# A fused retention and feed-forward block: small matmul tiles of two batches in one stretch, outputs in banks of their own, another order behind it

## The reference

```python
xn = layernorm(x)                                   # no weights
q, k, v = xn @ Wq, xn @ Wk, xn @ Wv                 # 8 heads of 16 features
# retention, in chunks of 64 tokens, gamma differs by head:
attn = einsum('bhid,bhjd->bhij', qc, kc) * D        # D[i,j] = gamma**(i-j) for i >= j, else 0
o_intra = einsum('bhij,bhje->bhie', attn, vc)
o_inter = einsum('bhid,bhde->bhie', qc * decay_q, S)
S = decay_s * S + einsum('bhjd,bhje->bhde', kc * decay_k, vc)
o = (o_intra + o_inter) @ Wo
h = ternary(w_fc) * scale applied to xn + gate * (xn @ v.T @ fast_b.T @ u.T)
y = ternary(w_proj) * scale applied to relu(h) ** 2
out = x + o + y
```

## Time and profile before

| what | value |
|---|---|
| median of 3 runs | 129.23 us (128.18 to 129.38) |
| the profiled execution's own time | 129.01 us |
| its span, first to last instruction | 127.0 us |
| granted TensorE clock, mean | 0.997 |
| PE busy | 117.0 us (92%) |
| DVE busy | 99.2 us (78%) |
| ACT busy | 78.7 us (62%) |
| POOL busy | 64.0 us (50%) |
| the chain that ended last | PE 80%, DVE 10%, issue 4%, ACT 2%, POOL 1% |

### The profile page before, as it was taken

How to read it: one execution, slowest core, us unless ns; L and a number is a source line. 1 busy time by engine, 2 the same in 40 slices (tenths; PEclk the granted TensorE clock), 3 DMA queues, 4 the chain that set the end, 5 groups by cost and what they waited for, 6 DMA issues and landing times.

```text
span 127.0 us, 6564 instructions
## 1 busy us (share of the span) xinstructions
PE 117.0 (92%) x2860; PEld 92.8 (73%) x2860; DVE 99.2 (78%) x261; ACT 78.7 (62%) x158; POOL 64.0 (50%) x60
## 2 busy tenths in 40 slices
PE   4979999988999999499999999999999999499991
PEld 4425869856688778377788778878897889377890
DVE  0788795489799969858699979896999799729832
ACT  3265669967871897227972897188738774382910
POOL 7099803984439161923439252916193529544400
PEclk9999999999999999999999999999999999999998
DMA  3849920000023000400023001300020002000202
GB/s 105 296 149 320 389 92 34 0 3 5 8 90 81 5 0 23 145 7 0 0 92 74 0 0 53 112 0 0 0 83 0 0 0 83 0 5 0 88 5 83
DMA packets 3357, 7.71 MB, mean 61 GB/s; under 512 B 384, under 2 KB 896, under 8 KB 3216
## 3 DMA queue, kind: packets, MB, share of 16 engines
q1 hardware_dynamic: 2880, 7.01, 16.3%
q10 hardware_dynamic: 464, 0.50, 1.2%
HBM read 5.42 MB, written 2.10 MB: 59 GB/s over the span
## 4 chain that ended last, share of the span: by engine, by line
PE 80%; DVE 10%; issue 4%; ACT 2%; POOL 1%; DVEq 0%; POOLq 0%
PE ps_work L659 10%; PE ps_score L735 8%; PE ps_work L663 7%; PE ps_work L660 7%; PE ps_score L705 6%; PE ps_score L747 5%; PE ps_score L781 5%; PE ps_y L761 4%; PE ps_y L762 4%; PE ps_score L720 3%; DVE sums_of L532 3%; PE ps_turn L668 3%; PE ps_y L765 2%; DVE xn L491 2%; PE ps_turn L692 1%
## 5 line engine op out<-in xcount | busy, mean ns | idle before, releaser
L300 POOL TENSOR_TENSOR sq_lo<-square,sq_hi 128x512 fp32r<-128x512 f32 x31 | 39.8, 1295 | 36.2 <-ACT sq_hi L356 36.2
L347 ACT ACTIVATE square<-ps_work 128x512 f32<-128x512 f32 x32 | 19.1, 596 | 23.1 <-PE ps_work L663 22.6
L516 DVE TENSOR_TENSOR scores<-ps_score,cst 128x512 f32<-128x512 f32 x32 | 20.3, 682 | 1.6 <-PE ps_score L705 1.6
L305 POOL TENSOR_TENSOR q_pair<-q_dec,cst 128x1024 f32<-128x1024 f32 x7 | 13.3, 1894 | 15.9 <-DVE q_dec L501 15.9
L356 ACT ACTIVATE sq_hi<-square 128x512 fp32r<-128x512 f32 x32 | 20.1, 627 | 0.1
L352 ACT ACTIVATE square<-square 128x512 f32<-128x512 f32 x32 | 18.9, 630 | 0.1
L491 DVE TENSOR_SCALAR xn<-x_in,mean_var,rstd 128x128 f32<-128x128 f32 x32 | 14.9, 528 | 0.3
L659 PE MATMUL ps_work<-xn_hi,w_hi 128*128 128x512 f32 x32 | 14.3, 447 | 0.4 <-issue 0.4
L735 PE MATMUL ps_score<-scores,v_pad 64*32 64x64 f32 x1024 | 12.5, 225 | 1.6 <-issue 1.6
L663 PE MATMUL ps_work<-xn_lo,w_hi 128*128 128x512 f32 x32 | 12.6, 394 | 0.0
L660 PE MATMUL ps_work<-xn_hi,w_lo 128*128 128x512 f32 x32 | 12.6, 393 | 0.0
(11 more groups left out here) (123 smaller groups left out, 238.6 us busy)
## 6 DMA issues: line engine op xcount, KB each, us to landing
x_in<-x_tok SPq DMA_DIRECT2D x8, 256.0 KB, 3.4
resid<-x_feat SPq DMA_DIRECT2D x1, 2048.0 KB, 7.7
out_feat<-resid SPq DMA_DIRECT2D x7, 256.0 KB
po_in<-ffn_weights SPq DMA_DIRECT2D x1, 320.0 KB, 3.2
fc_in<-ffn_weights SPq DMA_DIRECT2D x1, 256.0 KB, 3.7
q_table<-q_decay SPq DMA_DIRECT2D x1, 256.0 KB, 3.5
wqvk<-qvk_weights ACTq DMA_DIRECT2D x1, 192.0 KB, 3.9
cst<-const ACTq DMA_DIRECT2D x1, 129.0 KB, 3.9
```

Of the source, the lines that this page charges most:

```text
L300: nc.gpsimd.tensor_tensor(sq_lo[p][:, f, :], square[p][:, f, :], sq_hi[p][:, f, :].bitcast(F32), ALU.subtract).then_inc(lo_ready, 1)
L347: nc.scalar.activation(square[b.parity][:, f, :], ps_work[f % 2][:], ACT.Relu).then_inc(relu_ready, 1)
L516: nc.vector.tensor_tensor(scores[:, g].rearrange("p t s i -> p (t s) i"), ps_score[:, g].rearrange("p (a i) -> p a i", i=BLK), causal.unsq ...
```

## The change

The small tiles of two batches are put into one stretch: score(b), gather_states(b), own_values(b-1), carry(b-1). own_values moves a batch later, so there are two score tiles in SBUF (`scores` by parity). Outputs and states get two PSUM banks of their own (`ps_out`: the output in the first 256 columns of each, the states behind it); `ps_turn` and `ps_y` become banks 2 and 3 of `ps_score`, and keys and values of the tokens go to banks 0 and 1. All four hidden tiles stand ahead of the stretch. Behind it come the second product of b-1, the turned xn of b+1, the output product of b-1, and queries, keys and values of b+1. The queues of ScalarE and VectorE follow; GpSimd's and SyncE's stay. The waits change with the banks.

```diff
-        scores = sb("scores", [P, NG, NT, PAIR, BLK])
+        scores = [sb(f"scores{p}", [P, NG, NT, PAIR, BLK]) for p in range(2)]
...
         ps_score = pb("ps_score", [P, NG, SEQ])
+        ps_out = pb("ps_out", [P, ROWS, SEQ])
         ps_work = [pb(f"ps_work{p}", [P, SEQ]) for p in range(2)]
-        ps_turn = pb("ps_turn", [P, SEQ])
-        ps_y = pb("ps_y", [P, SEQ])
+        ps_turn, ps_y = ps_score[:, 2], ps_score[:, 3]
+        first_turn, ps_w1 = ps_out[:, 0], ps_out[:, 1]
...
             def body(b):          # ScalarE
                 take_relu(b, 0)
                 take_relu(b, 1)
                 root(b.step(1))
-                take_square(b, 0)
-                take_square(b, 1)
-                high_square(b, 0)
+                take_relu(b, 2)
+                take_relu(b, 3)
+                for f in range(3):
+                    take_square(b, f)
+                    high_square(b, f)
                 high_o(b.step(-1))
-                take_relu(b, 2)
-                high_square(b, 1)
                 round_xn(b.step(1))
-                take_relu(b, 3)
-                take_square(b, 2)
                 take_square(b, 3)
-                high_square(b, 2)
+                high_square(b, 3)
                 copy_k(b.step(1))
                 copy_k_tok(b.step(1), 0)
-                high_square(b, 3)
                 copy_k_tok(b.step(1), 1)
...
             def body(b):          # VectorE
                 before, after = b.step(-1), b.step(1)
                 statistics(after)
                 statistics_done(after)
-                take_states(before)
+                take_v(b, 1)
                 variance(after)
-                for k in range(3):
-                    add_states(before, k)
                 for step in range(4):
                     inverse_root(after, step)
                 normalise(after)
+                for g in MASK_ORDER:
+                    mask_scores(b, g)
                 low_o(before)
                 low_xn(after)
-                for g in MASK_ORDER[:2]:
-                    mask_scores(b, g)
+                take_states(b)
+                for k in range(3):
+                    add_states(b, k)
+                decay_q(after)
                 finish(before, ps_y)
-                decay_q(after)
-                for g in MASK_ORDER[2:]:
-                    mask_scores(b, g)
-                for side in range(2):
-                    take_v(after, side)
+                take_v(after, 0)
...
             def turn_xn(b):       # TensorE
                 pe.wait_ge(xn_ready, b.count(1, 1))
+                if b is not first:
+                    pe.wait_ge(scores_ready, b.count(NG, 1 - NG))
...
             def project_vk(b, side):
-                if side == 1 and b is first:
+                if b is not first:
+                    pe.wait_ge(scores_ready, b.count(NG, 0))
+                elif side == 1:
                     pe.wait_ge(q_ready, b.count(1, 1))
-                elif side == 1:
-                    pe.wait_ge(y_free, b.count(1, 0))
...
             def score(b):
                 pe.wait_ge(k_ready, b.count(1, 1))
                 pe.wait_ge(q_spread, b.count(PAIR, PAIR))
+                if b is not first:
+                    pe.wait_ge(v_ready, b.count(2, 2))
+                    pe.wait_ge(y_free, b.count(1, 0))
...
-            def body(b):
-                before, after = b.step(-1), b.step(1)
+            def all_hidden(b):
                 pe.wait_ge(q_ready, b.count(1, 1))
                 hidden(b, 0)
                 pe.wait_ge(k_ready, b.count(1, 1))
-                hidden(b, 1)
-                pe.wait_ge(v_ready, b.count(2, 2))
+                for f in range(1, NF):
+                    hidden(b, f)
+
+            def small_tiles(b):
+                before = b.step(-1)
+                pe.wait_ge(scores_ready, before.count(NG, NG))
+                pe.wait_ge(state_ready, before.count(1, 1))
+                score(b)
+                gather_states(b)
+                own_values(before)
+                carry(before)
+
+            def body(b):
+                before, after = b.step(-1), b.step(1)
+                all_hidden(b)
+                small_tiles(b)
+                pe.wait_ge(scores_ready, b.count(NG, 2))
                 second_product(before, ps_y, range(NF))
-                carry(before)
-                hidden(b, 2)
-                hidden(b, 3)
                 turn_xn(after)
                 pe.wait_ge(o_lo_ready, before.count(1, 1))
-                score(b)
                 output_product(before, ps_y)
                 project_q(after, b)
                 project_k(after, b)
                 project_vk(after, 0)
                 project_vk(after, 1)
-                gather_states(b)
-                own_values(b)
...
             before = last.step(-1)
-            pe.wait_ge(q_ready, last.count(1, 1))
-            hidden(last, 0)
-            carry(before)
-            pe.wait_ge(k_ready, last.count(1, 1))
-            hidden(last, 1)
-            pe.wait_ge(v_ready, last.count(2, 2))
-            second_product(before, ps_y, range(0, 2))
+            all_hidden(last)
+            small_tiles(last)
+            pe.wait_ge(scores_ready, last.count(NG, 2))
+            second_product(before, ps_y, range(NF))
             pe.wait_ge(o_lo_ready, before.count(1, 1))
-            score(last)
-            second_product(before, ps_y, range(2, NF))
+            own_values(last)
             output_product(before, ps_y)
-            hidden(last, 2)
-            for _ in range(6):
-                mm(ps_turn[0:GW, 0:1], ident[0:GW, 0:GW], ident[0:GW, 0:1], start=True, stop=True)
-            gather_states(last)
-            hidden(last, 3)
-            pe.wait_ge(relu_ready, last.count(NF, 3))
             last_second(0)
             last_second(1)
-            own_values(last)
             carry(last)
             last_second(2)
             last_second(3)
```

More of the change, by code:

```diff
@@ L204, in v_slots, with turn_bank @@
             return v.rearrange("p t g (s e) -> p (t g) s e", e=DK)[:, :, 0:4:3, :]
+        def turn_bank(b):
+            return first_turn if b is first else ps_turn
         def vk_bank(b, side):
-            other = ps_work[0] if b is first else ps_y
-            return (ps_turn if side == 0 else other)[:].rearrange("p (w t d) -> p w t d", w=2, t=2)
+            if b is first:
+                bank = first_turn if side == 0 else ps_work[0][:]
+            else:
+                bank = ps_score[:, side]
+            return bank.rearrange("p (w t d) -> p w t d", w=2, t=2)
         def by_block(o):
             return o[:].rearrange("p (t r i) -> p t r i", r=ROWS, i=BLK)
-        o_bank = ps_score[:, 0:ROWS, 0:NT * BLK].rearrange("p r (t i) -> p t r i", i=BLK)
+        o_bank = ps_out[:, :, 0:NT * BLK].rearrange("p r (t i) -> p t r i", i=BLK)
+        state_bank = ps_out[:, :, NT * BLK:NT * (BLK + GW)]
         first, last = Batch(0, 0), Batch(NB // 2 - 1, 1)
         HALF = SEQ // 2
-        last_banks = [ps_turn, ps_work[0]]
+        last_banks = [ps_score[:, 0], ps_score[:, 1]]
         last_cols = [slice(last.index * SEQ + h * HALF, last.index * SEQ + (h + 1) * HALF) for h in range(2)]
@@ L496, in low_xn @@
                 dve.wait_ge(xn_hi_ready, b.count(1, 1))
-                nc.vector.tensor_tensor(xn_lo[:], ps_turn[:], xn_hi[:].bitcast(F32), ALU.subtract).then_inc(xn_lo_ready, 1)
+                nc.vector.tensor_tensor(xn_lo[:], turn_bank(b), xn_hi[:].bitcast(F32), ALU.subtract).then_inc(xn_lo_ready, 1)
             def decay_q(b):
@@ L543, in finish @@
                 cols = bass.ds(b.index * SEQ, SEQ)
-                nc.vector.scalar_tensor_tensor(out=resid[:, cols], in0=bank[:], scalar=scale[:, NF:NF + 1],
+                nc.vector.scalar_tensor_tensor(out=resid[:, cols], in0=bank, scalar=scale[:, NF:NF + 1],
                                                in1=resid[:, cols], op0=ALU.mult, op1=ALU.add).then_inc(y_free, 1)
@@ L598, in _ @@
             nc.vector.tensor_tensor(wo_lo[:], ps_y[:, 0:D], wo_hi[:].bitcast(F32), ALU.subtract).then_inc(y_free, 1)
+            take_states(first)
+            for k in range(3):
+                add_states(first, k)
             take_v(after, 0)
-            take_v(after, 1)
             dve.wait_ge(resid_loaded, 16)
@@ L632, in _ @@
             before = last.step(-1)
-            take_states(before)
-            for k in range(3):
-                add_states(before, k)
-            low_o(before)
+            take_v(last, 1)
             for g in MASK_ORDER:
                 mask_scores(last, g)
-            finish(before, ps_y)
+            low_o(before)
             take_states(last)
@@ L647, in _ @@
                                     ALU.subtract).then_inc(last_low_ready, 1)
+            finish(before, ps_y)
             dve.wait_ge(o_done, last.count(1, 1))
@@ L734, in own_values @@
                                 rows = slice(r * BLK, (r + 1) * BLK)
```

(17 more changed lines are left out.)

63 lines of the change are left out of this document (33 added, 30 removed).

## The result

The kernel after takes 140.43 us, the median of four runs (139.83 to 144.58), where the kernel before on the same chip takes 128.70 (127.69 to 129.38). The ratio is 1.090, with a 95% interval of 1.078 to 1.103. Some executions of every kernel here take some per cent longer than the others; they stand in the medians, and the ratios leave them out. I had forecast 131.8 and a range up to 133.3: the direction was right, the size was not.

A forecast was written before the change was run, and what follows sets the result against it. TensorE's queue was taken as the bound. Five batches at +0.70 gave +3.5, ahead of the loop 0, behind it -0.7: +2.8 on 129.01 us makes 131.8, range 128.2 to 133.3.

The forecast's parts named there:

- The pause of 1.64 inside own_values at 53.97: TensorE idle in the profile of before, no cause shown; left in at 1.64 us, could also go or come twice.
- Borders: TensorE's changes of tile shape: two large-small borders of 0.20 us saved, two new small-small ones at 0.10 each, per batch.
- the 4.0 that I had named as a sign of being wrong: Stretch of small tiles on TensorE: the forecast is wrong if it takes less than 4.0 us.
- The rival that went by the Trainium skill's drain at a change of tiling: TensorE drains at every change of small shape: circle 13.91 us, +3.8, total 132.8; chance 0.12.
- Wait one: Third of four hidden tiles in a row waits for ScalarE's relu: 0.16 us plus 0.11 restart, 0.27 a batch.
- Wait two: Turned xn to queries: third term 2.04 us after the transposes began; 0.45 lost and about 0.11 restart.
- TensorE's circle: Sum of TensorE's pieces over one batch in the loop: 13.71 us against 13.06, +0.65.
- VectorE and GpSimd: They hold each other up: normalise ends at T + 10.5, masks 11.8, a second circle of 13.8 us, T being the transposes' start.
- A batch in sum: One batch in the loop: 13.76 us, +0.70 against before.
- The rival with waits half as long: Relu and xn waits half as long, VectorE not held: 13.25 us a batch, +0.3, total 129.3; chance 0.25.
- Ahead and behind: Outside the loop: 0 ahead, give or take 1 us; -0.7 behind, between -1.2 and 0.
- The upper end of the range: Total with borders at 0.20 and one more us ahead of the loop: 133.3 us.

The follow-up runs named there:

- run 1: Kernel after with TensorE's loop written out, same instructions and order: 155.2 us, ratio to before 1.197.
- run 2: Kernel before with TensorE's loop written out: 133.69 us, ratio to before 1.034.
- run 3: Kernel before with 17 more narrow warm-up products and one wide one less, shifting later instructions by 64: 136.52 us, ratio to before 1.055.
- run 4: Kernel after with 25 more narrow warm-up products and one wide one less, shifting later instructions by 96: 144.3 us, ratio to before 1.107.
- run 5: Kernel before, warm-up unchanged, with 16 narrow products on zeros behind the first transposes, a shift of 64 instructions: 135.29 us, ratio to before 1.049.
- run 6: Kernel after, warm-up unchanged, with 24 narrow products on zeros behind the first transposes, a shift of 96 instructions: 143.68 us, ratio to before 1.120.
- run 8: Run 7 with the last batch's small groups set apart by large matmuls: 137.1 us, ratio to before 1.063.
- run 9: Run 8 with ScalarE's high part of o behind the last batch's third relu instead of the first square: 133.81 us, ratio to before 1.038.
- run 10: Run 7 with carry and own_values moved behind the first hidden tile, in loop and last batch; o's parts earlier: 137.12 us, ratio to before 1.067.
- Run 7: Kernel after with the turned xn's transposes moved ahead of the second product: 137.82 us, ratio to before 1.075.

## Why the prediction failed

**The step that failed** is the last one on the ends: "The pause of 1.64 inside own_values at 53.97, put to nothing that the profile shows, I leave in; it could also go, or come twice." It came six times, 9.41 us in place of 1.64. The step failed because the term was carried over without a cause. The pause was no stray event but the visible end of a limit on TensorE's instructions, and the change works straight into it: the longest run of small tiles goes from 368 instructions (gather_states and own_values, 1.94 us) to 608 (all four groups, 3.96 us), while two packets of 256 start no less than 3.4 us apart. Written-out loops, moved borders and groups set apart (runs 1 to 6, 8 to 10) all move the pauses as this says. With the clock that falls behind the last of them it is 9.3 of the 10.8 us. The profile of before had two signs: an idle of 1.64 in the middle of 128 equal matmuls, and the queue "instruction" on the page.

**Borders.** Forecast: 0.10 for each new one. Measured: nothing. Score takes 1.13 to gather_states (75.23 to 76.36), and the whole stretch 3.96 (75.23 to 79.19), 0.23 less than the 4.19 of my terms and under the 4.0 that I had named as a sign of being wrong. I had read a border of 0.20 out of the 1.60 from own_values to carry. The single matmuls of that row in the trace show that it isn't there: the step from the last of own_values to the first of carry is 0.15 us, the same as from own_values to a large matmul at 68.27. The longest step inside own_values is 0.12, at instruction 5602, beside 5601, which leaves 225, as the pauses behind the loop do in runs 3, 5 and 10; that it is a block's border is likely and not shown. The rival that went by the Trainium skill's drain at a change of tiling (TensorEngine Tiling, Key Properties) asked for 0.40 here; no drain shows between these shapes, while the border of large and small tiles kept its 0.09 and 0.34.

**Wait one.** Forecast 0.27; measured 0.16 + 0.11 (73.24, 73.63, 73.97), exactly the row of batch 0.

**Wait two.** Forecast third term at 2.04; measured 2.01. Run 7 takes it away and saves 0.55 a batch, of 0.56 with the restart.

**TensorE's circle.** Forecast 13.71; measured 13.47, and the 0.24 are the borders' 0.20 and rounding.

**VectorE and GpSimd.** var_eps was due at T + 6.7 and came at 6.81, held to 7.5; the first Newton step took 0.74 where the next takes 0.16. The Trainium skill (SBUF — State Buffer, Who interferes with whom) had it that the small ones are held too; the trace agrees, with the 0.74. Normalise came at T + 9.14, not 9.4, and the masks at 10.17, not 10.5, so this circle did not reach past TensorE's: two masks are done at 77.86 + 1.28 = 79.14, and the second product starts at 79.19. A tie, as forecast, but at 13.5.

**A batch in sum.** Forecast +0.70 against before, or 13.76. Measured 13.47 to 13.53 against 13.19 on average from batch 4 to 7 (39.56 over three; 40.45 after): +0.30. The rival with waits half as long (+0.19) came nearest in size, though for another reason: the waits were whole, the borders free. The forecast of this term is more than twice what it measured. Of the 0.40 between, about 0.24 are the circle, 0.05 the tie, and 0.13 the base: I had 13.06 for the kernel before, which runs at 13.19 on average.

**Ahead and behind.** Without pauses and clock the change costs 1.5 ahead of batch 2's transposes (forecast 0, within 1) and saves 1.3 behind batch 7's (forecast 0.7, within 1.2). Ahead, hidden(1, 2) waits 0.73 for relu and score(1) 1.01 for take_v, the two places named, against 1.2 of waits there before. Another 0.4 stands there already at the first transposes (8.45 for 8.07), and run 9, with the same start, has them at 8.15; the rest was not separated. Behind, the wait of 1.61 for the states went, as said.

So all other terms together give 1.5 us for 2.8, in part by terms that cancel. With the 9.3 of pauses and clock put in, the forecast's sum would have been 141.1; but the trace of before shows one pause at one border, and the size of the six could not have been read from it. The upper end of the range has a slip: with borders at 0.20 and one more us ahead, 5 x 0.85 - 0.7 + 1 on 129.01 is 133.6, not 133.3, which changes nothing here.

## What to carry to other kernels

Count instructions, not only microseconds: where a run of small matmuls passes 256 matmuls and weight loads in less than the distance of two instruction packets (here 3.4 us), and the code isn't a repeated pass of a loop, TensorE can come to a stand, so place large matmuls between small groups in prologues, first passes and last batches. A single unexplained pause in a dense row can be a limit touched, and a change that makes the row denser must be priced for it. And since such a pause depends on where the blocks' borders fall, a difference of a few us between two orders can be alignment alone: shift both by some instructions before believing it.

## What the runs showed of the hardware

- TensorE's instructions come in packets of 16 KB for 256. In the twelve traces two of them never start less than 3.34 us apart (3.34 in run 4, 3.39 in run 2, 3.41 in before and after), and work resumes 1.2 to 1.6 us after a packet has ended.
- A pass of this loop has 1,396 recorded matmuls and weight loads, and in the second and third pass no packet comes. The Trainium skill ("Runtime: NRT & Kernel Launch", Instruction fetch mechanics) gives TensorE room for 2,048, which agrees; its advice that unrolled code is preferable does not hold here: writing the loop out cost 5 us in before (4.2 against its runs beside it) and 14.8 in after.
- Behind a stall TensorE's clock can drop to 1.2 GHz in spite of dense work: after the pause of 2.17 in after, after the wait of 2.59 in run 10, and in run 6 behind a run of narrow products. A wait then costs more than its length. The length of the pause alone does not tell: at the same instruction, 1473, the pause of 2.43 in run 3 is followed by 0.57 from 47 to 51 us, the one of 2.44 in run 5 by 1.00 from 46 to 50. In run 9 it was 0.50 from 52 to 54 us, behind a pause of 2.04, and 1.00 from 56 us to the end, where its one pause is 0.70.
- On VectorE three additions of 128x224 took 1.25 us with GpSimd idle (after, at 70.01) and 3.78 beside it (run 10); an operation on 128x4 took 0.74 beside it and 0.16 with it idle (after, 75.66 and 76.43).
